# A graph-network layer on one core: the prologue's small transfers are replaced, and a partition reads four consecutive chunks of destinations in one run

## The reference, cut to what matters

```python
def reference(x, src, dst, edge_attr_128, W1, b1, W2, b2, W3, b3, ln_w, ln_b):
    h = jnp.maximum(_layernorm(x, axis=-1), 0.0)               # 12500 x 128
    agg = jax.ops.segment_sum(edge_attr_128, dst, num_segments=12500)
    h = jnp.concatenate([h, agg], axis=-1)
    h = jax.nn.relu(h @ W1 + b1)                               # W1 256 x 128
    h = jax.nn.relu(h @ W2 + b2)
    h = h @ W3 + b3
    mu = jnp.mean(h, axis=-1, keepdims=True)
    var = jnp.mean(jnp.square(h - mu), axis=-1, keepdims=True)
    return x + (h - mu) * jax.lax.rsqrt(var + 1e-5) * ln_w + ln_b
```

## Time and profile before

| | before |
|---|---|
| median of 3 runs | 314.24 us (314.18 to 314.75) |
| the profiled execution | 314.22 us |
| its span in the profile | 312.4 us |
| PE busy | 280.1 us (90%) |
| DVE busy | 233.1 us (75%) |
| ACT busy | 156.8 us (50%) |
| POOL busy | 134.0 us (43%) |
| DMA | 116.50 MB, mean 373 GB/s |

### The profile page before, as it was taken

How to read it: one execution, slowest core, us unless ns; L and a number is a source line. 1 busy time by engine, 2 the same in 40 slices (tenths; PEclk the granted TensorE clock), 3 DMA queues, 4 the chain that set the end, 5 groups by cost and what they waited for, 6 DMA issues and landing times.

```text
span 312.4 us, 12913 instructions
## 1 busy us (share of the span) xinstructions
PE 280.1 (90%) x3955; PEld 182.3 (58%) x3955; DVE 233.1 (75%) x879; ACT 156.8 (50%) x413; POOL 134.0 (43%) x203
## 2 busy tenths in 40 slices
PE   2959999999999999999999999999999999999992
PEld 0746666656666666666556656565556565655671
DVE  4954777788787778777788777777787777777754
ACT  1442445555555545455555544545545545455533
POOL 7735334444444344444444443334444433444510
PEclk9976999999999999999999999999999999999998
DMA  7999999999999999999999999999999999999996
GB/s 237 342 377 373 373 373 372 372 376 383 383 383 383 383 383 384 383 383 384 383 383 383 383 383 382 384 384 383 382 383 383 383 383 383 384 382 384 384 392 217
DMA packets 83284, 116.50 MB, mean 373 GB/s; under 512 B 7116, under 2 KB 83272, under 8 KB 83272
## 3 DMA queue, kind: packets, MB, share of 16 engines
q1 hardware_dynamic: 82368, 116.06, 103.9%
q10 hardware_dynamic: 904, 0.28, 0.4%
HBM read 109.92 MB, written 6.40 MB: 372 GB/s over the span
## 4 chain that ended last, share of the span: by engine, by line
SPq 36%; PE 28%; issue 13%; DVE 11%; ACT 5%; DMA 4%; ACTq 1%; DVEq 1%
SPq L344 19%; SPq L379 13%; PE part_ps L497 10%; PE place_ps L508 7%; DVE onehot L973 4%; PE hid_ps L531 4%; ACT h L736 4%; PE hid_ps L541 3%; DMA ring<-in_edge_attr 3%; SPq L339 2%; DVE agg L1065 1%; DMA dst_i<-in_dst 1%; DVE x_mv L954 1%; DVE x_shift L966 1%; SPq L388 1%
## 5 line engine op out<-in xcount | busy, mean ns | idle before, releaser
L899 POOL TENSOR_SCALAR place<-iota,rows_at 128x128 f32<-128x128 f32 x130 | 84.4, 650 | 136.3 <-PE place_ps L508 127.8
L497 PE MATMUL part_ps<-ring,onehot 128*32 128x128 f32 x3120 | 113.7, 280 | 7.5 <-DMA ring<-in_edge_attr 3.2
L497 PEld LDWEIGHTS part_ps<-ring,onehot 128*32 128x32 f32 x3120 | 78.6, 110 | 66.1 <-issue 40.1
L1065 DVE TENSOR_TENSOR agg<-place_ps,agg 128x128 f32 x130 | 37.8, 291 | 58.6 <-PE place_ps L508 56.4
L508 PE MATMUL place_ps<-place,part 128*128 128x128 f32 x260 | 64.0, 329 | 2.9 <-ACT part L722 2.9
L973 DVE TENSOR_TENSOR onehot<-iota,local_t 128x768 f32<-128x768 f32 x65 | 62.4, 961 | 0.1
L736 ACT ACTIVATE h<-xs,x_shift,x_rstd 128x128 f32 (+2 forms) x98 | 41.3, 483 | 32.8 <-DVE x_shift L966 32.6
L508 PEld LDWEIGHTS place_ps<-place,part 128*128 128x128 f32 x260 | 39.5, 191 | 30.0 <-issue 21.5
L722 ACT ACTIVATE part<-part_ps 128x128 f32<-128x128 f32 x130 | 34.6, 267 | 25.3 <-PE part_ps L497 25.3
L907 POOL TENSOR_TENSOR xs<-xs,vecs 128x384 f32 (+2 forms) x33 | 33.6, 1019 | 27.0 <-ACT h L736 27.0
L531 PE MATMUL hid_ps<-agg,w1a 128*128 (+2 forms) x64 | 28.8, 532 | 7.3 <-DVE agg L1065 7.3
(11 more groups left out here) (103 smaller groups left out, 203.9 us busy)
## 6 DMA issues: line engine op xcount, KB each, us to landing
ring<-in_edge_attr SPq DMA_DIRECT2D x260, 384.0 KB, 8.2
xs<-in_x SPq DMA_DIRECT2D x32, 192.0 KB, 7.6
out_x<-xs SPq DMA_DIRECT2D x8, 384.0 KB
out_x<-xs SPq DMA_DIRECT2D x104, 24.0 KB
dst_i<-in_dst SPq DMA_DIRECT2D x1, 768.0 KB
out_x<-xs SPq DMA_DIRECT2D x2, 192.0 KB
tail_e<-in_edge_attr SPq DMA_DIRECT2D x1, 192.0 KB, 5.1
out_x<-xs SPq DMA_DIRECT2D x1, 168.0 KB
```

The lines of the kernel that those rows point to most:

```text
L497: last = nc.tensor.matmul(part_ps[par_q % 2][s * WIN:(s + 1) * WIN, 0:D], onehot[:, oct_par, first + s, j, :], e[:, s, j * D:(j + 1) * D], ...
L899: nc.gpsimd.tensor_scalar(place[:, par_q % 2, :], iota[:, 0:P], rows_at[:, k:k + 1], None, ALU.is_equal).then_inc(place_ready, 1)
L1065: nc.vector.tensor_tensor(v, place_ps[par_q % 2][:, 0:P], v, ALU.add).then_inc(added, 1)
```

## The change

The destinations of 512 chunks are now loaded as `dst_i[p, t, :]` = chunk `4 p + t`, so that a partition's four rows are one run of 6144 B in memory. A table `t` therefore holds every fourth chunk, and ACT's copies of the transposed tables (`least_row`, `local_t`) write with a step of four elements, which puts the chunks back in order. The two small loads of the fifth table move from SP to ACT, behind the three vectors. `tail_i` is gone: its destinations come from the fifth table's transposed copy, with the tail's own least subtracted, so the tail's one-hot rows shrink from 128 to 32 columns, and the sum is added to `agg` at a register's position. The two biases are loaded as rows of 512 B; PE turns each into a column with a matmul against a one, and ACT copies both to SBUF, after `normalise(0)`. DVE makes the first two one-hot octets later, behind the statistics of the last group of `x`, and waits for four tables of `local_t` and not for one. PE makes 13 and not 15 of the matmuls whose result nobody reads (`SPARE`).

```diff
-SPARE = 15
+SPARE = 13
-WTS = 6 * 16
+WTS = 4 * 16
...
                 full = (ROWT - 1) * P
                 sp.dma_start(dst_i[:, 0:ROWT - 1, :],
-                             dst[0:full * CHUNK].rearrange("(t p k) -> p t k", p=P, k=CHUNK)).then_inc(dst_loaded, 16)
-                sp.wait_ge(dst_padded, 1)
-                sp.dma_start(dst_i[0:LROW, ROWT - 1, :],
-                             dst[full * CHUNK:CHUNKS * CHUNK].rearrange("(p k) -> p k", k=CHUNK)).then_inc(dst_loaded, 16)
-                sp.dma_start(dst_i[LROW:LROW + 1, ROWT - 1, :],
-                             dst[TAIL0:EDGES].rearrange("(p k) -> p k", k=CHUNK)).then_inc(dst_loaded, 16)
-
-                sp.dma_start(tail_i[:, :], dst[TAIL0:EDGES].rearrange("(p j) -> p j", j=PER)).then_inc(tail_dst_loaded, 16)
+                             dst[0:full * CHUNK].rearrange("(p t k) -> p t k", t=ROWT - 1, k=CHUNK)).then_inc(dst_loaded, 16)
...
                 pe.wait_ge(local_t_ready, ROWT)
+                pe.wait_ge(vecs_ready, 1)
+                pe.wait_ge(bias_loaded, 2 * 16)
+                for k in range(2):
+                    last = nc.tensor.matmul(y_ps[:, 3 * D + k:3 * D + k + 1], bias_row[0:1, k, :], signs[0:1, 0, 0:1], start=True, stop=True)
+                last.then_inc(bias_spread, 1)
...
-                        last = nc.tensor.matmul(place_ps[1][:, 0:P], tail_e[:, j, :], tail_onehot[:, j, :],
+                        last = nc.tensor.matmul(place_ps[1][:, 0:WIN], tail_e[:, j, :], tail_onehot[:, j, :],
...
+                full = (ROWT - 1) * P
+                act.wait_ge(dst_padded, 1)
+                act.dma_start(dst_i[0:LROW, ROWT - 1, :],
+                              dst[full * CHUNK:CHUNKS * CHUNK].rearrange("(p k) -> p k", k=CHUNK)).then_inc(dst_loaded, 16)
+                act.dma_start(dst_i[LROW:LROW + 1, ROWT - 1, :],
+                              dst[TAIL0:EDGES].rearrange("(p k) -> p k", k=CHUNK)).then_inc(dst_loaded, 16)
...
-                for t, a in ((w1x, w1[0:P, :]), (w1a, w1[P:2 * P, :]), (w2s, w2), (w3s, w3),
-                             (b1s, b1.rearrange("(p o) -> p o", o=1)), (b2s, b2.rearrange("(p o) -> p o", o=1))):
+                for t, a in ((w1x, w1[0:P, :]), (w1a, w1[P:2 * P, :]), (w2s, w2), (w3s, w3)):
                     act.dma_start(t[:, :], a).then_inc(wts_loaded, 16)
+                for k, a in enumerate((b1, b2)):
+                    act.dma_start(bias_row[0:1, k, :], a.rearrange("(o f) -> o f", o=1)).then_inc(bias_loaded, 16)
...
-                nc.scalar.activation(least_row[0:1, 0:4 * P], part_ps[0][0:1, :], ACT.Copy)
+                nc.scalar.activation(least_row[0:1, 0:(ROWT - 1) * P].rearrange("o (p t) -> o p t", t=ROWT - 1),
+                                     part_ps[0][0:1, :].rearrange("o (t p) -> o p t", t=ROWT - 1), ACT.Copy)
...
-                    nc.scalar.activation(local_t[:, :, t * P:(t + 1) * P],
+                    rest = local_t[:, :, (ROWT - 1) * P:NCOL]
+                    whole = local_t[:, :, 0:(ROWT - 1) * P].rearrange("p j (s t) -> p t j s", t=ROWT - 1)
+                    nc.scalar.activation(whole[:, t, :, :] if t < ROWT - 1 else rest,
...
                 normalise(0)
+                act.wait_ge(bias_spread, 1)
+                nc.scalar.activation(biases[:, :], y_ps[:, 3 * D:3 * D + 2], ACT.Copy).then_inc(biases_ready, 1)
+                act.wait_ge(biases_ready, 1)
...
-                dve.wait_ge(local_t_ready, 1)
-                make_onehot(0, 0, free=False)
-                make_onehot(1, 1, free=False)
                 dve.wait_ge(least_row_ready, 1)
...
                 mean_x(LAST)
+                dve.wait_ge(local_t_ready, ROWT - 1)
+                make_onehot(0, 0, free=False)
+                make_onehot(1, 1, free=False)
...
-                dve.wait_ge(tail_dst_loaded, 16)
-                nc.vector.tensor_scalar(tail_local[:, :], tail_i[:, :], float(TAIL_BASE), None, ALU.subtract).then_inc(tail_rebased, 1)
+                nc.vector.tensor_copy(tail_local[:, :], local_t[:, :, CHUNKS]).then_inc(tail_rebased, 1)
...
-                nc.vector.tensor_tensor(tail_onehot[:, :, :], iota[:, 0:P].unsqueeze(1).to_broadcast([P, PER, P]),
+                nc.vector.tensor_tensor(tail_onehot[:, :, :], iota[:, 0:WIN].unsqueeze(1).to_broadcast([P, PER, WIN]),
...
-                    v = agg[:, TAIL_BASE:NODES]
-                    nc.vector.tensor_tensor(v, place_ps[1][:, 0:P], v, ALU.add).then_inc(tail_added, 1)
+                    v = agg[:, bass.ds(bases(QUADS, 1)[0], WIN)]
+                    nc.vector.tensor_tensor(v, place_ps[1][:, 0:WIN], v, ALU.add).then_inc(tail_added, 1)
```

More of the change, by code:

```diff
@@ L45 @@
 DONE = CHUNKS * CHUNK - TAIL0
-TAIL_BASE = NODES - P
 OCT = 2 * QC
@@ L85 @@
 STORED_EARLY = 13
[L86 removed]
+WTS = 4 * 16
 def gnn_kernel(nc, x, dst, edges, w1, b1, w2, b2, w3, b3, lnw, lnb, out):
[L90 removed]
+    assert CHUNKS == (ROWT - 1) * P + LROW and GROUPS == 32 and QUADS == 4 * STEPS + AHEAD and LAST_P * LAST_PER == LAST_N and LAST_P <= P and TOP_QUADS * QC == (ROWT - 1) * P and 0 < FIRST_OF_LAST <= LROW and RC * RP == REST
     with ExitStack() as ctx:
@@ L108, in gnn_kernel @@
         tail_e = sb("tail_e", [P, PER, D])
-        tail_i = sb("tail_i", [P, PER], I32)
         tail_local = sb("tail_local", [P, PER])
-        tail_onehot = sb("tail_onehot", [P, PER, P])
+        tail_onehot = sb("tail_onehot", [P, PER, WIN])
         iota = sb("iota", [P, BANK])
@@ L133, in gnn_kernel @@
         w3s = sb("w3s", [P, P])
-        b1s = sb("b1s", [P, 1])
-        b2s = sb("b2s", [P, 1])
+        bias_row = sb("bias_row", [1, 2, D])
+        biases = sb("biases", [P, 2])
+        b1s, b2s = biases[:, 0:1], biases[:, 1:2]
         vec_row = sb("vec_row", [1, 3, D])
@@ L178, in gnn_kernel @@
         vec_spread = sem("vec_spread")
+        bias_loaded = sem("bias_loaded")
+        bias_spread = sem("bias_spread")
+        biases_ready = sem("biases_ready")
         vecs_ready = sem("vecs_ready")
```

10 lines of the change are left out of this document (5 added, 5 removed).

## The result

| | before | after |
|---|---|---|
| median | 314.69 us (313.84 to 316.02, 19 runs) | 315.84 us (313.72 to 318.12, 19 runs) |
| after / before | | 1.0031, 95% interval 1.0016 to 1.0045 |
| the profiled execution, its span | 314.22, 312.4 us | 316.84, 315.1 us |

The change makes the kernel about 1.0 us slower, where 0.9 us faster was forecast, and its times scatter twice as widely. The profiled execution is the fourth longest of its kernel's 19, 2.62 us above that of before, so it shows the loss larger than the median has it.

A forecast was written before the change was run, and what follows sets the result against it. The DMA engines were taken to bound the whole run; savings of 0.32 + 0.39 + 0.2 = 0.91 us gave 313.3 us from 314.24, with 2.3 us of later prologue hidden. The range was 312.5 to 314.8 us.

The forecast's parts named there:

- The first reserve: Compute side's lead in the edge ring: 5.5 us, 4.6 after the DMA gain, forecast as not reached.
- The DMA sum: DMA engines' work removed ahead of the last edge load: 0.91 us, bounds 0.3 and 1.4.
- The dip at 5 us: Low DMA rate between 4.4 and 5.4 us, where `tail_i` passes: 0.32 us lost, to go with its packets.
- The long packets: Destination loads of 512 chunks in a quarter of the packets: 0.2 us gained, bounds 0 and 0.63.
- the second reserve: DMA work ahead of the first edge load waiting for the third quad: 4.0 us, 3.1 with faster engines.
- The queue, +0.6: Small destination loads on ACT's queue land later, delaying DVE's passes by 0.6 us; bounds -0.2 and +1.2.
- The tables, +1.0: ACT's copies with a step of four and later one-hot octets on DVE: `row_at` 1.0 us later.
- The biases, +0.3: ACT's copy of the biases ahead of the first part copies: 0.3 us later, PE's bias matmuls long done.
- The register load, +0.7: Tail's position loaded into a DVE register before the third quad: 0.7 us later, from 0.3 to 1.4.
- Rival (D): Late prologue empties the DMA engines at the third quad's reload; lateness beyond 3.1 us lost, up to 314.9 us; chance 0.17.
- (B): Destinations' slow start goes with long packets: sum 1.3 to 1.5 us, time 312.6 to 312.9 us; chance 0.15.
- (C): Small packets cost little, dips come from elsewhere: gain 0.3 to 0.6 us, time 313.65 to 313.95; chance 0.26.

The follow-up runs named there:

- b3: Kernel before, with two idle DVE passes of 2.15 us each ahead of the first pass, no transfer changed; ratio to before 1.0021.
- e12: Kernel after, with the two small destination loads back on SP and one idle DVE pass ahead of the first; ratio to before 1.0043.
- a1: Kernel after, unchanged, run and profiled a second time; ratio to before 1.0025.
- b1: Kernel before, with only the two small destination loads moved from SP's to ACT's queue; ratio to before 0.9992.
- e3: Kernel after, with table layout, contiguous copies and one-hot order of before, small loads still on ACT; ratio to before 0.9982.
- e4: Kernel before, with only the small packets removed: biases as rows, tail's destinations taken from `local_t`; ratio to before 0.9980.
- e1: Kernel after, with the two small destination loads back on SP behind the long load; ratio to before 0.9991.
- e14: Same kernel as e4, run a second time; ratio to before 0.9988.
- e13: Kernel after, with only PE's two bias matmuls moved ahead of its first two quads; ratio to before 1.0014.
- e11: Kernel after, with the two small destination loads issued on ACT ahead of the three vectors; ratio to before 1.0015.
- e9: Kernel after, with PE's bias matmuls moved ahead of its first two quads and no unread matmuls (`SPARE = 0`); ratio to before 1.0039.
- e2: Kernel after, with PE's wait for the tail's addition moved behind the third quad's matmuls; ratio to before 1.0041.

## Why the prediction was wrong

**What bounds the kernel** was read rightly. The DMA engines' work ahead of the last edge load sets the end: the step at 294.24 us moved by +2.61 where the balance of rates gave +2.26, and by +1.51 (b3) and +2.13 (e12) where it gave 1.1 and 2.1. The first reserve, of 5.5 us on the compute side, was never the limit: as forecast, PE waits less often for the ring, 21 times and 14.5 us in place of 31 and 21.5.

```profile
PEld part_ps L491 <- DMA ring<-in_edge_attr: 14.5, 21, 0.8
```

The prediction had also said what would show it wrong, a stretch between 25 and 35 us under 360 GB/s, and that is what came.

**The DMA sum** was right in size, 0.91 us against 0.80 in the profile after and 0.67 in a1, and partly wrong in its parts. The dip at 5 us was put down to the tail's 128 packets. When b1 took the two small loads off SP's queue and left those packets, the rate from 4 to 6 us rose from 317 to 368 GB/s (51 x 2 / 373 = 0.27 us); taking the packets too, in e3, brought 390 (0.12 us). I had costed the move at nothing for the DMA engines. Over the first 25 us little of it stays, though: 324 GB/s in b1 against 322, 0.13 us. The biases: from 13 to 15 us 312 became 369 in e4, 0.31 us, but the next four us carry 373 and no longer 387, which takes 0.15 back. From 8 to 16 us the four profiles with the bias packets have 336 to 353 GB/s, the fourteen without 358 to 367, so this term is the best borne out, at 0.2 to 0.4 us. The long packets: 334 GB/s in the first 25 us with them, 331 in e3 without, 0.2 us as taken; but the eight profiles with them on ACT have 329 to 335, so no gain of theirs is shown. On SP (e1, 325) they showed none over e4 and e14 (330 and 325) either.

**The step that failed is the comparison of the lateness with the second reserve.** "Sum: 0.6 + 1.0 - 0.3 + 0.3 + 0.7 = 2.3 us later at the third quad", against "3.1 when the engines are 0.9 faster". The sum measured 4.75 us in the profile after and 2.99 in a1; the reserve measured 2.1 to 2.5. Both sides were off:

- The queue, +0.6: measured +1.8 in the profile after, +0.3 to +1.9 over the eleven. The vector of the earlier trace rows was a fair model for the least of it, and its scatter could not be seen in one profile.
- The tables, +1.0: +0.91. ACT's strided copies took about 0.9 us and not 0.7, but the row that they delay, the one-hot octets, did not wait for all of it; the strided copy of `least_row` cost nothing.
- The tail's one-hot rows, -0.3: 0.26 us in place of 0.56, as said, but it brought nothing on the path: the flag is 13.14 us behind `least` with either.
- The biases, +0.3: ACT's copy with its wait holds the first part copy for 0.83 us and puts the addition 0.56 us back where PE has time, as in e1. Where PE is at half clock, as in the kernel after, its bias matmuls, costed as "long done", stand in front of the branch and take 1.01 us, and PE's queue comes last.
- The register load, +0.7: 0.40 us of issue time, 0.44 in all.
- Not in the sum: PE's clock. In the profile after it is at the lower level from 18 to 34 us. It accounts for 0.45 us between `least` and flag, and with the bias and unread matmuls for 0.54 behind it. The parts then add up: 1.82 + 0.94 + 0.45 + 0.56 + 0.44 + 0.54 = 4.75 us.
- The reserve, 3.1: the rates fall between additions at 25.86 and 26.28 us, so it is 2.1 to 2.5; for the transfers of before, 4.0 by the prediction, b3 gives about 3.0. What the subtraction left out is that each following quad must come in time too, every 2.1 us at 373 GB/s, and they come 2.17 us apart at the lower clock and once 2.83 at the full one. That this is the whole of the missing us is not shown.

Rival (D) named the place, the mechanism and the threshold's kind, and got 0.17; its own numbers (3.1 us, then one for one) ask for 4.0 us of lateness to lose the gain, where e13 and e11, at 2.7 and 2.8, already had. With bounds of 0.2 to 4.7 around the sum and 3.1 as the limit, a third of that span lay beyond it. The chance should have been near that, and the range should not have ended at 314.8, below (D)'s own 314.9. Even 314.9 would not have held the 315.84 that came, since the reserve was smaller than (D) had it.

(B) and (C) are not what happened. (C) is right in size for its own term, 0.3 to 0.6 us: e4 and e14 put the small packets at 0.6 and 0.4 us. That the dips come from elsewhere holds for the one at 5 us in part, and not for the one at 14 us.

Left open: e9's median; and why the profiles of e3, e9, e14, e13 and e2 have their step 0.9 to 1.4 us later than the rates up to 45 us give. A difference of 1 GB/s over the remaining 250 us is 0.7 us, and the stretches are printed no finer than that.

## What to carry to other kernels

When transfers are the bound, look for the first reload that waits for computing, and count from issue to landing how much work the engines have ahead of it; everything that delays the prologue is drawn from that reserve, free until it is gone. Test the reserve by itself with an idle instruction ahead of the first one on the path: two such kernels told more here than all sums. Follow the queue order of the engines too: a small copy on ACT can delay an addition on DVE that never reads it. And of a change that bundles several edits, run the one that removes transfers alone: here it is 0.4 to 0.6 us faster, if barely clear of the noise, and the rest took more than that back.

## What the runs showed that I had not expected

- A DMA of 12 KB and one of 1.5 KB, issued on ACT's queue at 1.9 and 2.2 us (1.3 and 1.9 in e11) behind 786 KB issued on SP's, were waited for until 6.1 to 7.75 us, and differently in every profiled execution; on SP's queue, behind the same load, until 5.3 to 6.1.
- Those same small DMAs, of eight partitions and of one, go with a dip on SP's queue ahead of the edges: from 4 to 6 us the seven profiles with them there have 260 to 347 GB/s, the ten with them behind the vectors on ACT 358 to 390, and e11 has 329. The 128 packets of 12 B are not needed for it: e1 and e12 lack them and have 295 and 260.
- ACT's copy of 128 x 384 from PSUM took 0.49 us with a contiguous destination, about 0.9 with a step of four float32. The Trainium skill (SBUF — State Buffer, section "Door 1: The DMA port swizzle") has the penalty for a new 16-byte line at every access, without its size; the trace agrees with it for 128 partitions. It doesn't for the copy of 512 elements on one partition, which took 0.59 us either way.
